# Moving the cast for the high part of the transposed memory from VectorE to ScalarE in a decoder layer

## What is computed

```python
x = x + attn(layernorm(x))                       # 16 heads, scores * exp(-0.01*|i-j|), softmax
q = layernorm(x) @ W.T + b                       # cross-attention
logits = q @ ctx.T + (1 - mask) * -1e6           # [1024, 6404]
x = x + softmax(logits) @ ctx
x = x + ffn(layernorm(x))                        # 4-bit block quantization before each product
```

## Time and profile before

| | |
|---|---|
| median of three runs | 594.06 us |
| span of the profiled execution | 594.0 us, 9035 instructions |
| busy: TensorE / VectorE / ScalarE / GpSimd | 499.6 / 421.8 / 299.8 / 133.4 us |
| exponentials of the self-attention (L523) | 256 of 0.596 us, 139.1 us |
| diagonal products (L748) | 128 of 0.319 us, 40.8 us |

### The profile page before, as it was taken

How to read it: one execution, slowest core, us unless ns; L and a number is a source line. 1 busy time by engine, 2 the same in 40 slices (tenths; PEclk the granted TensorE clock), 3 DMA queues, 4 the chain that set the end, 5 groups by cost and what they waited for, 6 DMA issues and landing times.

```text
span 594.0 us, 9035 instructions
## 1 busy us (share of the span) xinstructions
PE 499.6 (84%) x3228; PEld 322.3 (54%) x3228; DVE 421.8 (71%) x1031; ACT 299.8 (50%) x596; POOL 133.4 (22%) x125
## 2 busy tenths in 40 slices
PE   5363869979999999999977998979899797989953
PEld 5120113323333333345355997979789797878851
DVE  5876998988999999989566436665646576654343
ACT  2062006645766767677725572736546272737420
POOL 5701950089000000000034322221312222210000
PEclk9575557988999999999999998999989899999995
DMA  2048244420600430001046532423232432400000
GB/s 61 0 140 260 43 100 98 100 63 2 158 5 3 126 98 1 3 1 39 0 176 194 161 100 83 131 81 111 85 107 86 116 111 75 139 14 5 2 6 4
DMA packets 20133, 45.90 MB, mean 77 GB/s; under 512 B 3876, under 2 KB 9192, under 8 KB 19512
## 3 DMA queue, kind: packets, MB, share of 16 engines
q1 hardware_dynamic: 19864, 44.77, 26.6%
q0 software_dynamic: 224, 0.54, 0.3%
HBM read 40.39 MB, written 4.72 MB: 76 GB/s over the span
## 4 chain that ended last, share of the span: by engine, by line
PE 62%; DVE 28%; DMA 3%; issue 3%; ACT 2%; POOL 1%; SPq 0%; DVEq 0%; ACTq 0%; POOLq 0%
PE banks L869 42%; PE banks L966 9%; DVE banks L672 9%; PE banks L1096 6%; PE banks L955 3%; DVE xn L620 2%; DVE logits L776 2%; DVE fa L811 1%; DMA operands<-key_parts 1%; PE banks L978 1%; DVE banks L748 1%; DVE fa L812 1%; ACT probs L523 1%; DVE qc_lo L730 1%; DVE fa L807 1%
## 5 line engine op out<-in xcount | busy, mean ns | idle before, releaser
L523 ACT ACTIVATE probs<-banks 128x512 f32<-128x512 f32 x256 | 139.1, 596 | 108.8 <-PE banks L955 106.5
L869 PE MATMUL banks<-operands 96*128 96x512 bf16 (+5 forms) x704 | 150.4, 346 | 23.4 <-DMA operands<-key_parts 13.4
L672 DVE CUSTOM_DVE_ANT_0 banks<-banks,decay 128x1024 f32<-128x1024 f32 x128 | 156.4, 1226 | 14.9 <-PE banks L869 11.0
L869 PEld LDWEIGHTS banks<-mem,pT 128*128 128x128 f32 (+1 forms) x816 | 108.5, 195 | 7.9
L869 PE MATMUL banks<-mem,pT 128*128 128x128 f32 (+1 forms) x816 | 112.0, 280 | 0.0
L869 PEld LDWEIGHTS banks<-operands 96*128 96x128 bf16 (+1 forms) x704 | 59.3, 100 | 88.0 <-DVE row_max L672 24.7
L776 DVE CUSTOM_DVE_ANT_0 logits<-banks,mring 128x512 f32<-128x512 f32 (+1 forms) x102 | 67.4, 668 | 48.9 <-PE banks L869 23.3
L545 ACT ACTIVATE pT<-banks 128x512 f32<-128x512 f32 (+1 forms) x104 | 60.4, 581 | 52.9 <-PE banks L1096 52.9
L427 POOL TENSOR_SCALAR mring<-mring 128x1024 f32<-128x1024 int32 (+1 forms) x55 | 52.6, 956 | 90.6 <-DMA mring<-in_mask_BxSxS_ik 88.4
L966 PE MATMUL banks<-probs,v_ext 128*32 128x512 f32 x512 | 70.5, 624 | 0.7 <-ACT probs L523 0.7
L869 PE MATMUL banks<-memT_hi,qc_hi 128*128 128x512 f32 (+1 forms) x104 | 50.6, 486 | 19.1 <-DVE cmax L776 19.1
(11 more groups left out here) (161 smaller groups left out, 518.7 us busy)
## 6 DMA issues: line engine op xcount, KB each, us to landing
mring<-in_mask_BxSxS_ik SPq DMA_DIRECT2D x47, 512.0 KB, 3.5
operands<-query_parts SPq DMA_DIRECT2D x24, 192.0 KB
operands<-key_parts SPq DMA_DIRECT2D x24, 192.0 KB
key_parts<-operands SPq DMA_DIRECT2D x10, 256.0 KB, 4.7
query_parts<-operands SPq DMA_DIRECT2D x4, 384.0 KB, 4.8
mring<-in_mask_BxSxS_ik SPq DMA_DIRECT2D x8, 130.0 KB, 2.1
operands<-shift_parts SPq DMA_DIRECT2D x48, 4.0 KB, 1.7
x_sb<-in_x SPq DMA_DIRECT2D x1, 512.0 KB, 4.1
```

Of the source, the lines that this page charges most:

```text
L523: act.activation(probs[:, (gb % 2) * HG + h, :], PS[:, u % 3, :], ACT.Exp).then_inc(s_p, 1)
L672: dve.tensor_tensor_reduce(out=rows, in0=rows, in1=decay[:, off:off + S], scale=1.0, scalar=-3.0e38, op0=ALU.mult, op1=ALU.max, accum_out= ...
L869: return pe.matmul(o, a, b, start=start, stop=stop)
```

## The change

ScalarE gets a function `mem_high(c)` with the cast and the waits that stood ahead of it, called after the second exponential of a pair, for the same chunk that VectorE works on after the diagonal product of the same pair. In VectorE's `mem_parts` the cast and those waits are gone; it still waits for `s_mhi`, which ScalarE now raises, and then subtracts.

```diff
+            def mem_high(c):
+                k0, kw = chunk(c)
+                act.wait_ge(s_mt, c + 2)
+                if c == 0:
+                    act.wait_ge(s_st, 3 * 2 * BLKS)
+                act.activation(memT_hi[:, k0:k0 + kw], PS[:, 4 + c % 4, 0:kw], ACT.Copy).then_inc(s_mhi, 1)
+
@@ for h in range(HG): ... act.activation(probs[...], ACT.Exp)
                         if h % 2 == 1:
+                            if 0 <= 2 * (gb - MEM_BLOCK) + h // 2 - 1 < NC:
+                                mem_high(2 * (gb - MEM_BLOCK) + h // 2 - 1)
                             attn_step(0, early_turn(2 * (gb - EARLY_BLOCK) + h // 2))
@@ def mem_parts(c):
                 src = PS[:, 4 + c % 4, 0:kw]
-                dve.wait_ge(s_mt, c + 2)
-                if c == 0:
-                    dve.wait_ge(s_st, 3 * 2 * BLKS)
-                dve.tensor_copy(memT_hi[:, k0:k0 + kw], src).then_inc(s_mhi, 1)
                 dve.wait_ge(s_mhi, c + 1)
                 dve.tensor_tensor(memT_lo[:, k0:k0 + kw], src, memT_hi[:, k0:k0 + kw].bitcast(F32),
                                   ALU.subtract).then_inc(s_mlo, 1)
```

## The result

The changed kernel took 613.79 us (median of four runs, 610.15 to 615.71), the kernel before 594.39 beside it: 1.032 times as long, 95% interval 1.028 to 1.036. In a later session it took 611.80 against 593.25, 1.031 (1.027 to 1.034). The profiled execution has a span of 610.5 us, and its time was 612.24: here and in every later run with a profile the time is 1.7 us above the span. Lines have moved by a few: the shift is L960 (before L955), the diagonal product L753 (L748), the subtraction L700 (L695), the exponential L530 (L523), the cast L520 on ScalarE.

A forecast was written before the change was run, and what follows sets the result against it. TensorE and VectorE were taken as both nearly full in the stretch, with the order of waits deciding. Forecast: 594.06 + 16.5 (waits at full clock) + 2.3 (clock) = 612.9 us, range 608.8 to 618.0.

The forecast's parts named there:

- The ring of 2.83 us per half block: Blocks 54 to 59: exponentials, cast, subtraction, diagonal product and shift wait in a closed loop, 2.83 us against 1.54 before.
- The first handoff, 1.66 us late: First shift of block 54 begins at 271.01 instead of 269.35 us, behind the first cast and subtraction: 1.66 us late.
- Twelve links less the short chunk, 33.5: First shift of block 54 to that of block 60: 12 x 2.83, less 0.5 for the 260-column chunk; 18.52 us before.
- The 0.2 off in block 60: In block 60 TensorE no longer waits for an exponential before its scores: 0.2 us less.
- The sum of 16.5 at the full clock: Added time over the stretch and block 60 with TensorE at full clock: 1.66 + 15.0 - 0.2 = 16.5 us.
- The clock, 2.3 us: TensorE's gaps in the six blocks lower its clock: a third of 6.8 us, so 2.3 us more, ends 0 and 6.8.
- Rival 1: The closed loop of waits with TensorE at full clock throughout: 610.6 us, chance 0.27.
- Rival 2: The closed loop of waits with the clock at 1.2 GHz for nearly the whole stage: 617.4 us, chance 0.12.
- Rival 3: Throughput alone: the diagonal product goes ahead, ScalarE sets blocks of about 3.5 us; 2.6 us more, 596.7, chance 0.05.
- Rival 4: Not slower: casts fit ScalarE's 0.86 us idle per block, early enough for VectorE; 593.8 us, chance 0.04.

The follow-up runs named there:

- The wait alone: Kernel before, cast left on VectorE, each cast made to wait until both exponentials of the same pair of units are done: 617.38 us, 1.040.
- the two broken rings: Changed kernel with ScalarE's casts one pair of units earlier, 595.33 us; changed kernel with VectorE's subtractions one pair later, 594.42 us.
- the kernel with added transposes: Changed kernel with the four transposes of each chunk done twice (even chunks) or three times (odd ones): 611.09 us.
- the 13 copies added: Kernel before plus 13 copies of 128 x 512 on ScalarE at the places of the casts, nobody waiting for them in the stretch: 594.03 us, 1.001.
- the early cast: Changed kernel with ScalarE's cast of each chunk one pair of units earlier: 595.33 us, 1.003.

## Why the prediction was right, point by point

- **The ring of 2.83 us per half block** was right to the hundredth (271.24 to 274.07), link by link: cast 0.60, product to shift 0.06, shift to exponential 0.26. The wait alone and the two broken rings show that the order makes it, not the work.
- **The first handoff, 1.66 us late:** 1.67. **Twelve links less the short chunk, 33.5:** 33.48 with the clock held. **The 0.2 off in block 60:** 10.45 instead of 10.66 us to the last shift. The sum of 16.5 at the full clock is 1.66 + 14.96 - 0.21 = 16.4 in the trace of the kernel with added transposes. That kernel's median is 17.8 above before, though. The other 1.4 us can't be placed by traces, since the parts outside the stretch scatter by more than that, and I have no cause for them.
- **The clock, 2.3 us:** 2.6 and 1.8 in the two profiles, but the agreement is partly luck, as two errors cancel. The term was priced for the stretch alone, and there it was too large: only 1.0 and 0.5 us fell there. The forecast doubled TensorE's 1.89 us to 3.8 for the half block with the value product at 1.2 GHz; measured it is 284.68 - 281.31 = 3.37, without a gap, where the ring takes 2.83. The other half block hides the low clock almost whole: the short last one took 304.49 - 302.08 = 2.41 us at 1.2 GHz against 2.35 in the kernel with added transposes. By these rows the low level throughout would cost about 6 x (0.54 + 0.06) = 3.6 us, not 6.8 (an estimate), and a third of it 1.2. What made up for it is a cost that the sum didn't have: 1.6 and 1.4 us behind the stretch, nearly all in block 60, which TensorE sets itself, so that nothing hides its longer matmuls. That block took 4.05 us in the one profile and 3.82 in the other, against 2.52 at the full clock. Two shifts and three stretches of TensorE alone in the kernel after (length, busy, clock, transfers):

```profile
281.31 0.29 PE L960 MATMUL banks<-operands,ones_rows 99*128 99x128 bf16 x1 [1.50 <-DVE banks L753]
284.68 0.24 PE L960 MATMUL banks<-operands,ones_rows 99*128 99x128 bf16 x1
```
```profile
278.00:280.00 2.00, 1.33 (x9) 1.00 0.00 0
...
282.00:284.00 2.00, 2.00 (x13) 0.50 0.00 0
...
306.00:308.00 2.00, 2.00 (x14) 0.50 0.00 0
```

- The Trainium skill tells of a clock that swings with short idle times between groups of matmuls ("TensorE: Matmul & The Clock Gate", section "A second HAM failure mode: psum-queue depth-cycling"). The traces agree: the clock fell with gaps of at most 1.50 us, and with the gaps filled it stayed at 1.00 through the stretch. That ScalarE is closer to PSUM, as the Trainium skill says ("Advanced Engine Details and Errata", section "TRN2 Errata"), agrees with the price, 0.60 against 0.68 us, and decided nothing.
- **Rival 1**, the full clock throughout, is what the added transposes made; the changed kernel itself had two falls in each of its profiles. **Rival 2** was not seen. **Rival 3** was mispriced: throughput alone costs 0.38 us, not 2.6. Its price had a wait for the shift in every block, and with the 13 copies added ScalarE waited for a shift only once, for 0.7 us. **Rival 4** needs the cast ahead of VectorE, and with the early cast the time came back to within 0.3% of before; but its gain of 0.3 us wasn't there, as ScalarE had become as full as TensorE and the copy of the head outputs came late.

## What to carry to other kernels

When work is moved to an engine with idle time, write down what stands behind the instruction that now waits for it, on the engine that gave the work away. If the receiving engine's next input is behind that wait, the engines form a ring, and each round takes the sum of all links. Here that was 1.29 us more per half block for a cast of 0.60. Putting the producer one step earlier or the consumer one step later took nearly the whole price off. Three engines that are each half idle and wait for one another in turn are how such a ring looks in a profile.

## What was new about the hardware

With idle gaps of 0.94 and 1.50 us in turn, and TensorE busy for 3.22 of 5.66 us, the clock went on at 2.4 GHz for 11 us in one profile (270 to 281) and for 17 in the other (270 to 287) before it fell. This first time it stayed low for about 3.4 us in both. It fell again at about 298 us in the one, then for some 10 us, and at about 305 in the other. The stretches around the first fall of the second profile (length, then PE, PEld, DVE, ACT, POOL, clock, transfers):

```profile
286.00:288.00 2.00, 0.64 (x5) 0.65 (x6) 0.90 (x2) 1.24 (x3) 0.00 (x0) 0.88 0.00 0
288.00:290.00 2.00, 2.00 (x12) 0.46 (x10) 0.77 (x2) 1.20 (x3) 0.00 (x0) 0.50 0.03 8
```

The ten runs of the changed kernel part into two groups by mean clock: seven at 0.895 to 0.898 took 609.77 to 612.30 us, three at 0.885 to 0.887 took 614.15 to 615.71. The groups' means differ by 3.8 us. Where in those three the clock was low isn't known, as none of them was profiled. For the gaps of the ring speaks that the kernel before has no mean clock under 0.894 in 57 runs, and that the wait alone, with the same kind of ring, has 0.886 or 0.887 in all four. But the kernel before scatters as much in time, from 589.48 to 596.15 us in 17 runs on one chip, and there too the shortest run has the highest mean clock (0.909) and the longest the lowest (0.896). That such gaps make a kernel's time less steady isn't shown.
